# A state-space tokenizer before attention and a feed-forward layer: part of its chunk loop moved from VectorE and ScalarE to GpSimd

## The chip, the cores and the metric

The kernel runs on one NeuronCore of a Trainium2 chip, as one launch. The metric is device microseconds of one execution; lower is better. The median of three runs of the kernel before is given below. The profile is of one further execution, taken by the hardware profiler.

## What is computed

The reference is a vision tower's one layer: a tokenizer that builds the hidden states, then `h + attention(layernorm(h))` (local, landmark and global attention), then a feed-forward layer with block-wise quantized operands. The change lies in the tokenizer alone, which is, cut to what matters:

```python
C = x[..., 0] + 1j * x[..., 1]                    # (16, 256, 64)
B = B_ri[..., 0] + 1j * B_ri[..., 1]
A = -exp(inv_A_real) + 1j * A_imag
dt = exp(log_dt)
dtA = A * dt[:, None]
Ct = B[None] * C / (1.0 - dtA / 2) * dt[:, None]
dA = (1.0 + dtA / 2) / (1.0 - dtA / 2)
V = exp(log(dA)[:, :, None] * arange(512))         # (256, 64, 512)
h = 2.0 * einsum('chn,hnl->chl', Ct, V).real       # (16, 256, 512)
```

For every token h (256 of them) this is a product of the 16 x 64 coefficients with the 64 x 512 powers, in complex numbers.

## The kernel before

The whole program is a row of stages with a barrier of all engines between two of them: tokenizer, local attention, landmark attention, landmarks from tokens, landmark keys, global attention, feed-forward. Each stage has its own block of instructions per engine; in a stage the engines are tied by semaphores written out by hand. Nothing is scheduled by a planner: each engine runs its instructions in the order of the code, and a wait in front of an instruction holds back all that is behind it on that engine.

The tokenizer (`tokenizer`, from L115) splits the power l: with l = a + 64 b, a in 0..63 and b in 0..7, the power of a is the right operand of a matmul and the power of b is folded into the left one. The state index n and the two parts (real, imaginary) make the 128 partitions that are summed over. After a start that forms the parameters (VectorE, L293 to L349), transposes them and x (TensorE) and prepares the tables `X`, `Pb` (the coefficients times the powers of b, L382 to L387) and `ER` (the decay of the powers of a, L375, L240), the loop goes over 16 chunks (`NCH`) of 16 tokens (`CH`):

- ScalarE, `phases` (L247): 16 instructions of 64 elements, the turn a times omega of each token, into `ph`;
- ScalarE, `rounded` (L256): one instruction of 1024 elements that adds 1.5 x 2^23 to it, so that f32 rounds it to a whole number, into `nf`;
- VectorE, `fractions` (L394): takes the constant off again and subtracts `ph`, so `nf` holds the negative fraction of a turn (scalar_tensor_tensor, 1024 elements);
- ScalarE (L274): the sine of it, in place;
- VectorE: the left operands `L`, two products of 2048 elements for the two parts (L403, both operands broadcast, out of `X` and `Pb`) and their sum (L408);
- VectorE (L411): the right operands `R`, sine times decay, 1024 elements;
- TensorE (L442): 16 f32 matmuls of 128 x 128 by 128 x 64, one a token (each shows as two records), into two PSUM banks;
- ScalarE, `tokens` (L264): two copies of the banks to `hs`, and a DMA of 512 KB on SP's queue (L203) stores them to `h_s`.

`ph`, `nf`, `L`, `R`, `hs` and the pairs of banks have two buffers each. The orders on the engines are: VectorE `fractions(0)`, then for each chunk the two products, the sum, the decay product, `fractions(ch + 1)`; ScalarE `phases(0)`, `rounded(0)`, then for each chunk the sine, `phases(ch + 1)`, `rounded(ch + 1)`, `tokens(ch - 1)`. TensorE waits for `l_ready` and `r_ready` of a chunk before its first token. GpSimd has no instruction in this stage; it works in local attention (L724 to L742), global attention (L1752 to L1775) and the feed-forward layer (L2184).

Of the kernel before, what the change touches and what calls it, by code (L numbers as in the profile page):

```python
# [7 lines left out]
ALU = mybir.AluOpType  # L8
ACT = mybir.ActivationFunctionType
# [6 lines left out]
P = 128  # L16
BATCH = 16
# [17 lines left out]
ROUND = 1.5 * 2.0 ** 23  # L35
# [80 lines left out]
def tokenizer(nc, A, consts_d, h_d):  # L116


    CH = 16
    NCH = TOK // CH  # L120
    ctx = ExitStack()
    with ctx:
        def sb(name, shape, dt=F32):
            return ctx.enter_context(nc.sbuf_tensor(name, shape, dt))

        def sem(name):
            return nc.alloc_semaphore(name)
# [5 lines left out]
        aim = sb("tk_aim", [P, 2, NST])  # L133
        bri = sb("tk_bri", [P, 2, NST, 2])
        nat = sb("tk_nat", [P, 29, 2, NST])
        big = sb("tk_big", [P, 1])
        cst64 = sb("tk_c64", [P, 3, TOK])
        par = sb("tk_par", [P, 4, TOK])
        X = sb("tk_x", [P, 2, TOK, BATCH])
        ER = sb("tk_er", [P, TOK, 64])  # L140
        W = sb("tk_w", [P, 2, TOK, 8])
        Pb = sb("tk_pb", [P, 2, TOK, 8])
        L = sb("tk_l", [P, 2, 2, CH, P])

        WA, WB = (L[:, k, 0].rearrange("p t (m b) -> p (t m) b", b=8) for k in range(2))
        ph, nf = (xin[:, k].rearrange("p c n -> p (c n)").rearrange("p (u t a) -> p u t a", u=2, t=CH)
                  for k in range(2))
        R, hs = (W[:, k].rearrange("p t b -> p (t b)").rearrange("p (u t a) -> p u t a", u=2, t=CH)
                 for k in range(2))
# [22 lines left out]
        s_ev = sem("tk_ev")  # L172
        s_er0 = sem("tk_er0")
        s_er = sem("tk_er1")
        s_wph = sem("tk_wph")
        s_wsn = sem("tk_wsn")
        s_pb = sem("tk_pbd")
        ph_ready = sem("tk_ph_ready")
        rr_ready = sem("tk_rr_ready")
        nf_ready = sem("tk_nf_ready")  # L180
        sin_ready = sem("tk_sin_ready")
        r_ready = sem("tk_r_ready")
        l_ready = sem("tk_l_ready")
        mm_ready = sem("tk_mm_ready")
        hs_ready = sem("tk_hs_ready")
        out_done = [sem(f"tk_out_done{u}") for u in range(2)]
# [21 lines left out]
        @block.scalar  # L208
        def _(act):

            act.wait_ge(s_ld, 80)
            act.activation(nat[:, 0, 0, 0:2], ldt[:], ACT.Exp).then_inc(s_act, 1)
            act.activation(nat[:, 1], iar[:], ACT.Exp).then_inc(s_act, 1)

            act.wait_ge(s_nat, 1)
            act.activation(nat[:, 10], nat[:, 9], ACT.Ln).then_inc(s_act, 1)
            act.wait_ge(s_nat, 2)
            act.activation(nat[:, 11], nat[:, 12], ACT.Arctan).then_inc(s_act, 1)

            act.wait_ge(s_x, 32)  # L220
            for ri in range(2):
                for a in range(2):
                    src = xin[:, a].rearrange("p c (n r) -> p c n r", r=2)[:, :, :, ri]
                    for e in range(2):
                        ins = act.activation(xdup[:, ri, a, :, e * NST:(e + 1) * NST], src, ACT.Copy)
                    ins.then_inc(s_xd, 1)
            for k in range(16):
                ri, q, a = k // 8, k % 4, (k % 8) // 4
                act.wait_ge(s_xtr, k + 1)
                act.activation(X[:, ri, a * P:(a + 1) * P, 4 * q:4 * q + 4],  # L230
                               ps[(k + 2) % 8][:].rearrange("p (q t) -> p t q", q=4), ACT.Copy).then_inc(s_ev, 1)

            for w in range(2):
                act.wait_ge(s_wph, 2 + w)
                act.activation(W[:, w], W[:, w], ACT.Sin, scale=-TWO_PI, bias=tau[:, 1 + w:2 + w]).then_inc(s_wsn, 1)
            act.wait_ge(s_wph, 1)
            act.activation(WA, WA, ACT.Exp).then_inc(s_wsn, 1)
            for k in range(8):
                act.wait_ge(s_er0, k + 1)
                act.activation(ER[:, 32 * k:32 * k + 32], ER[:, 32 * k:32 * k + 32], ACT.Exp).then_inc(s_er, 1)  # L240

            def phases(ch):

                if ch >= 2:
                    act.wait_ge(nf_ready, ch - 1)
                for t in range(CH):
                    ins = act.activation(ph[:, ch % 2, t], c("iota_a"), ACT.Identity,  # L247
                                         scale=par[:, 1, ch * CH + t:ch * CH + t + 1], bias=c("off_r"))
                ins.then_inc(ph_ready, 1)

            def rounded(ch):

                act.wait_ge(ph_ready, ch + 1)
                if ch >= 2:
                    act.wait_ge(r_ready, ch - 1)
                act.activation(nf[:, ch % 2], ph[:, ch % 2], ACT.Identity, bias=big[:]).then_inc(rr_ready, 1)  # L256

            def tokens(ch):

                act.wait_ge(mm_ready, ch + 1)  # L260
                if ch >= 2:
                    act.wait_ge(out_done[ch % 2], 16 * (ch // 2))
                for k in range(2):
                    ins = act.activation(hs[:, ch % 2, 8 * k:8 * k + 8], ps[ch % 2 * 2 + k][:].rearrange(  # L264
                        "p (t a) -> p t a", t=8), ACT.Copy)
                ins.then_inc(hs_ready, 1)

            act.wait_ge(s_xd, 4)
            act.wait_ge(s_par, 2)
            phases(0)  # L270
            rounded(0)
            for ch in range(NCH):
                act.wait_ge(nf_ready, ch + 1)
                act.activation(nf[:, ch % 2], nf[:, ch % 2], ACT.Sin, scale=-TWO_PI  # L274
                               ).then_inc(sin_ready, 1)
                if ch + 1 < NCH:
                    phases(ch + 1)
                    rounded(ch + 1)
                if ch:
                    tokens(ch - 1)  # L280
            tokens(NCH - 1)

        @block.vector
        def _(dve):
            st = Steps(dve, s_dve)
# [3 lines left out]
                    n = st.mark(f(a))  # L289
                return n  # L290

            st.mark(dve.memset(big[:], ROUND))
            dve.wait_ge(s_act, 2)  # L293
            dt = nat[:, 0, 0, 0:2]
            hdt, ear, zr, zi = nat[:, 2, 0, 0:2], nat[:, 1], nat[:, 3], nat[:, 4]
# [95 lines left out]
            def fractions(ch):  # L391

                dve.wait_ge(rr_ready, ch + 1)
                dve.scalar_tensor_tensor(nf[:, ch % 2], nf[:, ch % 2], ROUND, ph[:, ch % 2], ALU.subtract, ALU.subtract  # L394
                                         ).then_inc(nf_ready, 1)

            fractions(0)
            for ch in range(NCH):
                t0, u = ch * CH, ch % 2
                if ch >= 2:  # L400
                    dve.wait_ge(mm_ready, ch - 1)
                for k in range(2):
                    ins = dve.tensor_tensor(L[:, u, k].rearrange("p t (c b) -> p t c b", b=8),  # L403
                                            X[:, k, t0:t0 + CH, :, None].to_broadcast([P, CH, BATCH, 8]),
                                            Pb[:, k, t0:t0 + CH, None, :].to_broadcast([P, CH, BATCH, 8]), ALU.mult)
                    st.mark(ins)
                st.wait(st.n)
                dve.tensor_tensor(L[:, u, 0], L[:, u, 0], L[:, u, 1], ALU.add).then_inc(l_ready, 1)  # L408
                dve.wait_ge(sin_ready, ch + 1)
                dve.wait_ge(s_er, ch // 2 + 1)  # L410
                dve.tensor_tensor(R[:, u], nf[:, u], ER[:, t0:t0 + CH], ALU.mult).then_inc(r_ready, 1)  # L411
                if ch + 1 < NCH:
                    fractions(ch + 1)

        @block.tensor
        def _(pe):

            pe.wait_ge(s_nat, 3)
            for a in range(2):
                for q in range(4):  # L420
                    ins = pe.transpose(ps[a][:, q * P:(q + 1) * P], dup4[:, q, a], ident)
                ins.then_inc(s_tr, 1)
            for k in range(16):
                ri, q, a = k // 8, k % 4, (k % 8) // 4
                pe.wait_ge(s_xd, ri * 2 + a + 1)
                if k >= 8:
                    pe.wait_ge(s_ev, k - 7)
                elif k >= 6:
                    pe.wait_ge(s_par, k - 5)
                for j in range(4):  # L430
                    ins = pe.transpose(ps[(k + 2) % 8][:, j * P:(j + 1) * P], xdup[:, ri, a, 4 * q + j], ident)
                ins.then_inc(s_xtr, 1)
            pe.wait_ge(s_ev, 16)
            for ch in range(NCH):
                u = ch % 2
                pe.wait_ge(l_ready, ch + 1)
                pe.wait_ge(r_ready, ch + 1)
                if ch >= 2:
                    pe.wait_ge(hs_ready, ch - 1)
                for t in range(CH):  # L440
                    o = ps[u * 2 + t // 8][:, (t % 8) * 64:(t % 8) * 64 + 64]
                    ins = pe.matmul(o, L[:, u, 0, t], R[:, u, t], start=True, stop=True)  # L442
                ins.then_inc(mm_ready, 1)
# [1937 lines left out]
```

## Time and profile before

| | us |
|---|---|
| median of 3 runs | 1784.9 (1778.79 to 1786.39) |
| the profiled execution | 1778.12 |
| its span, first to last instruction | 1776.3 |
| VectorE busy | 1307.3 (74%) |
| TensorE busy | 1508.6 (85%) |
| ScalarE busy | 1022.3 (58%) |
| GpSimd busy | 561.2 (32%), none of it in the tokenizer but four memsets at 0.3 us |
| tokenizer, up to its last store's issue | 0 to 224 |

The span is 1.8 us less than the execution's own time. TensorE's granted clock is 0.893 over the whole span, in tenths by slice of 44.4 us 8555569999999999999976689889999899999999; 0.50 is 1.2 GHz and 1.00 is 2.4 GHz. In rows of the trace the engines are PE (TensorE matmul), PEld (its weight load), DVE (VectorE), ACT (ScalarE), POOL (GpSimd) and SP; a trailing q is an engine's queue, and L442 is line 442 of the kernel. An engine's gap before an instruction stands in brackets with what ended it. x16 is a count of instructions merged into a row. The names of buffers are those of the memory that a tile lies in: `ph` and `nf` show as tk_xin, `R` and `hs` as tk_w.

### The profile page before, as it was taken

The numbers are of one execution on the slowest core, as the hardware profiler recorded it, in microseconds if no ns is written. First come the engines' busy times: TensorE is split into PE (matmuls) and PEld (weight loads), VectorE is DVE, ScalarE is ACT, GpSimd is POOL, SyncE is SP. The second block draws the span as 40 slices with busy tenths as digits, with TensorE's granted clock in tenths as the row PEclk, the third lists the DMA queues.
The fourth block names the chain that finished last, engine by engine and source line by source line (L and its number), as shares of the span: only waits on it lengthen the run. The fifth ranks groups of instructions, "written<-read, shape, count | busy, mean of one in ns | idle before, by whom it ended". The sixth has DMA issues, their size and how long they took to land. (4 is left out here: it accounts for less than half of the span.)

```text
span 1776.3 us, 33180 instructions
## 1 busy us (share of the span) xinstructions
PE 1508.6 (85%) x11568; PEld 1007.3 (57%) x11568; DVE 1307.3 (74%) x2414; ACT 1022.3 (58%) x2579; POOL 561.2 (32%) x584
## 2 busy tenths in 40 slices
PE   2177739999999999999958776679999589999997
PEld 2177726766776677667646755456666334444443
DVE  8999836777777777777614255169999579999997
ACT  7799627888778887888722133056776232333232
POOL 0000014445444444454400000025555523333333
PEclk8555569999999999999976689889999899999999
DMA  2022251222222222222230065345555124444443
GB/s 59 1 60 60 59 168 67 100 97 77 77 101 77 89 77 97 100 77 77 85 131 1 0 221 188 111 138 163 163 163 163 60 66 104 98 102 100 107 96 89
DMA packets 189649, 171.82 MB, mean 97 GB/s; under 512 B 120064, under 2 KB 121728, under 8 KB 189568
## 3 DMA queue, kind: packets, MB, share of 16 engines
q1 hardware_dynamic: 189568, 170.80, 32.7%
q8 instruction: 44, 0.72, 0.2%
q14 instruction: 37, 0.30, 0.1%
HBM read 94.21 MB, written 59.77 MB: 87 GB/s over the span
## 5 line engine op out<-in xcount | busy, mean ns | idle before, releaser
L1057 PE MATMUL al_ps<-al_w,al_xT 128*128 128x512 f32 (+2 forms) x1024 | 352.0, 498 | 0.0
L1057 PEld LDWEIGHTS al_ps<-al_w,al_xT 128*128 128x128 f32 x1024 | 192.6, 193 | 127.4 <-issue 107.3
L2184 POOL TENSOR_TENSOR ff_zq<-ff_z,ff_back 128x1024 bf16<-128x1024 fp8e4 x64 | 122.4, 1912 | 225.8 <-DVE ff_z L2207 225.8
L442 PE MATMUL tk_ps<-tk_w,tk_l 128*128 128x64 f32 x512 | 113.0, 422 | 79.5 <-DVE tk_w L411 52.4
L442 PEld LDWEIGHTS tk_ps<-tk_w,tk_l 128*128 128x128 f32 x512 | 110.4, 332 | 82.1 <-issue 82.1
L2151 ACT ACTIVATE ff_sg<-ff_gate 128x1024 f32<-128x1024 f32 x64 | 65.6, 1025 | 149.1 <-PE ff_gate L2230 149.1
L739 POOL TENSOR_TENSOR al_qv<-al_qv,al_qe 128x512 f32<-128x512 f32 x48 | 62.0, 1291 | 248.7 <-PE al_ps L1130 248.7
L2249 PE MATMUL ff_acc<-wdT,ff_zT 128*128 128x512 bf16 x512 | 122.5, 383 | 5.5 <-DMA ff_zT<-ff_zq 5.5
L2230 PE MATMUL ff_up<-wuT,xqT 128*128 128x512 bf16 x512 | 121.6, 380 | 3.0 <-DVE ff_z L2199 3.0
L2230 PE MATMUL ff_gate<-wgT,xqT 128*128 128x512 bf16 x512 | 121.9, 381 | 0.7 <-ACT ff_sg L2151 0.7
L993 DVE TENSOR_REDUCE al_mx<-al_ps 128x32 f32<-128x2048 f32 x32 | 73.3, 2292 | 58.1 <-PE al_ps L1130 58.1
L1994 PE MATMUL ag_ps<-ag_w,ag_aT 128*128 128x512 f32 x256 | 114.8, 602 | 0.0
L885 ACT ACTIVATE al_p<-al_ps,al_mx 128x64 f32<-128x64 f32 x512 | 107.8, 355 | 0.0
L724 POOL TENSOR_TENSOR al_qk<-al_r 128x512 f32<-128x512 f32 x64 | 81.7, 1288 | 68.1 <-DVE al_r L933 68.1
L1762 POOL TENSOR_TENSOR ag_a<-ag_a,ag_o 128x1024 f32<-128x1024 f32 x16 | 37.7, 2357 | 167.0 <-DVE ag_a L1913 167.0
L2249 PEld LDWEIGHTS ff_acc<-wdT,ff_zT 128*128 128x128 bf16 x512 | 50.1, 98 | 68.0 <-DMA ff_zT<-ff_zq 7.4
L247 ACT ACTIVATE tk_xin<-tk_cst,tk_par 128x64 f32<-128x64 f32 x256 | 86.3, 425 | 0.0
L2230 PEld LDWEIGHTS ff_gate<-wgT,xqT 128*128 128x128 bf16 x512 | 50.3, 98 | 62.4 <-issue 1.9
L2230 PEld LDWEIGHTS ff_up<-wuT,xqT 128*128 128x128 bf16 x512 | 45.0, 98 | 71.2 <-DVE ff_z L2199 25.4
L2199 DVE TENSOR_TENSOR ff_z<-ff_sg,ff_up 128x1024 f32<-128x1024 f32 x64 | 77.7, 1214 | 9.8 <-ACT ff_sg L2151 9.8
L2204 DVE TENSOR_TENSOR ff_zv<-ff_z,ff_inv 128x1024 f32<-128x1024 f32 x64 | 78.5, 1226 | 2.2
L1994 PEld LDWEIGHTS ag_ps<-ag_w,ag_aT 128*128 128x128 f32 x256 | 48.6, 195 | 54.8 <-issue 54.8
(311 smaller groups left out, 3413.3 us busy)
## 6 DMA issues: line engine op xcount, KB each, us to landing
al_hx<-h_s SPq DMA_DIRECT2D x36, 256.0 KB, 2.7
o_s<-al_o SPq DMA_DIRECT2D x32, 272.0 KB, 2.1
h_s<-tk_w SPq DMA_DIRECT2D x16, 512.0 KB, 3.8
v_s<-al_v SPq DMA_DIRECT2D x32, 256.0 KB, 2.1
k_s<-al_kT SPq DMA_DIRECT2D x32, 256.0 KB, 2.4
q_s<-al_qT SPq DMA_DIRECT2D x32, 256.0 KB, 2.6
lt_kT<-k_s SPq DMA_DIRECT2D x16, 512.0 KB, 4.6
lt_v<-v_s SPq DMA_DIRECT2D x16, 512.0 KB, 3.6
```

The costliest lines, as they stand in the source:

```text
L247: ins = act.activation(ph[:, ch % 2, t], c("iota_a"), ACT.Identity, scale=par[:, 1, ch * CH + t:ch * CH + t + 1], bias=c("off_r"))
L442: ins = pe.matmul(o, L[:, u, 0, t], R[:, u, t], start=True, stop=True)
L724: pool.tensor_tensor(qk[:, part * D:(part + 1) * D].rearrange("p (h d) -> p h d", d=DH), r1[:, heads], r2[:, heads], ALU.add).then_inc(out ...
L885: ins = act.activation(p[:, g, hd * S:(hd + 1) * S], ps[:, g, hd * S:(hd + 1) * S], ACT.Exp, bias=mx[:, 8 * g + hd:8 * g + hd + 1])
L993: dve.tensor_reduce(mx[:], ps[:, 0:4].rearrange("p b (h s) -> p (b h) s", s=S), AX.X, ALU.max, negate=True).then_inc(mx_r.sem, 1)
L1057: ins = pe.matmul(out, xT[:, T, k], w[:, k, cols], start=False, stop=True, skip_group_check=True)
L1994: ins = pe.matmul(out, aT[:, T, k], w[:, k], start=False, stop=True, skip_group_check=True)
L2184: pool.tensor_tensor(zq[:, u].rearrange("p (k s) -> p k s", s=QB), z8[:, u].rearrange("p (k s) -> p k s", s=QB), back[:, u, :, None].to_br ...
L2199: dve.tensor_tensor(z[:, u], sg[:, u], up[:].rearrange("p b n -> p (b n)"), ALU.mult).then_inc(z_r.sem, 1)
L2204: ls(dve.tensor_tensor(b3_(zv[:]), b3_(z[:, u]), inv[:, :, None].to_broadcast([P, NB, QB]), ALU.mult))
L2230: ins = pe.matmul(bank[:, n], K.xqT[:, k, bass.ds(t * P, P)], wT[:, k, (2 * hf + n) * D:(2 * hf + n + 1) * D], start=(k == 0), stop=(k == ...
L2249: ins = pe.matmul(acc[:, T], zT[:, u, k], K.wdT[:, 2 * KC * hf + k], start=False, stop=True, skip_group_check=True)
```

## The change

`CV = 13` splits a chunk's 16 tokens. VectorE forms the left operands of the first 13; GpSimd forms those of the last three (`left`: two products and their sum, on 384 elements each) with a semaphore of its own, `lp_ready`, which TensorE waits for in front of token 13. GpSimd also takes the product with the decay (for all 16 tokens) from VectorE, and the rounding from ScalarE (`rounded`, now a tensor_scalar with the constant as immediate, so that the tile `big` goes). ScalarE computes the phases two chunks ahead of the sine in place of one. GpSimd's order is `rounded(0)`, `rounded(1)`, `left(0)`, then for each chunk the decay product, `left(ch + 1)`, `rounded(ch + 2)`. The waits on buffers are those of before, moved with the work.

```diff
--- before.py
+++ after.py
@@ -117,6 +117,7 @@
 
 
     CH = 16
+    CV = 13
     NCH = TOK // CH
     ctx = ExitStack()
     with ctx:
@@ -133,7 +134,6 @@
         aim = sb("tk_aim", [P, 2, NST])
         bri = sb("tk_bri", [P, 2, NST, 2])
         nat = sb("tk_nat", [P, 29, 2, NST])
-        big = sb("tk_big", [P, 1])
         cst64 = sb("tk_c64", [P, 3, TOK])
         par = sb("tk_par", [P, 4, TOK])
         X = sb("tk_x", [P, 2, TOK, BATCH])
@@ -181,6 +181,8 @@
         sin_ready = sem("tk_sin_ready")
         r_ready = sem("tk_r_ready")
         l_ready = sem("tk_l_ready")
+        lp_ready = sem("tk_lp_ready")
+        s_pool = sem("tk_pool")
         mm_ready = sem("tk_mm_ready")
         hs_ready = sem("tk_hs_ready")
         out_done = [sem(f"tk_out_done{u}") for u in range(2)]
@@ -248,13 +250,6 @@
                                          scale=par[:, 1, ch * CH + t:ch * CH + t + 1], bias=c("off_r"))
                 ins.then_inc(ph_ready, 1)
 
-            def rounded(ch):
-
-                act.wait_ge(ph_ready, ch + 1)
-                if ch >= 2:
-                    act.wait_ge(r_ready, ch - 1)
-                act.activation(nf[:, ch % 2], ph[:, ch % 2], ACT.Identity, bias=big[:]).then_inc(rr_ready, 1)
-
             def tokens(ch):
 
                 act.wait_ge(mm_ready, ch + 1)
@@ -268,14 +263,13 @@
             act.wait_ge(s_xd, 4)
             act.wait_ge(s_par, 2)
             phases(0)
-            rounded(0)
+            phases(1)
             for ch in range(NCH):
                 act.wait_ge(nf_ready, ch + 1)
                 act.activation(nf[:, ch % 2], nf[:, ch % 2], ACT.Sin, scale=-TWO_PI
                                ).then_inc(sin_ready, 1)
-                if ch + 1 < NCH:
-                    phases(ch + 1)
-                    rounded(ch + 1)
+                if ch + 2 < NCH:
+                    phases(ch + 2)
                 if ch:
                     tokens(ch - 1)
             tokens(NCH - 1)
@@ -289,7 +283,6 @@
                     n = st.mark(f(a))
                 return n
 
-            st.mark(dve.memset(big[:], ROUND))
             dve.wait_ge(s_act, 2)
             dt = nat[:, 0, 0, 0:2]
             hdt, ear, zr, zi = nat[:, 2, 0, 0:2], nat[:, 1], nat[:, 3], nat[:, 4]
@@ -400,17 +393,54 @@
                 if ch >= 2:
                     dve.wait_ge(mm_ready, ch - 1)
                 for k in range(2):
-                    ins = dve.tensor_tensor(L[:, u, k].rearrange("p t (c b) -> p t c b", b=8),
-                                            X[:, k, t0:t0 + CH, :, None].to_broadcast([P, CH, BATCH, 8]),
-                                            Pb[:, k, t0:t0 + CH, None, :].to_broadcast([P, CH, BATCH, 8]), ALU.mult)
+                    ins = dve.tensor_tensor(L[:, u, k, 0:CV].rearrange("p t (c b) -> p t c b", b=8),
+                                            X[:, k, t0:t0 + CV, :, None].to_broadcast([P, CV, BATCH, 8]),
+                                            Pb[:, k, t0:t0 + CV, None, :].to_broadcast([P, CV, BATCH, 8]), ALU.mult)
                     st.mark(ins)
                 st.wait(st.n)
-                dve.tensor_tensor(L[:, u, 0], L[:, u, 0], L[:, u, 1], ALU.add).then_inc(l_ready, 1)
-                dve.wait_ge(sin_ready, ch + 1)
-                dve.wait_ge(s_er, ch // 2 + 1)
-                dve.tensor_tensor(R[:, u], nf[:, u], ER[:, t0:t0 + CH], ALU.mult).then_inc(r_ready, 1)
+                dve.tensor_tensor(L[:, u, 0, 0:CV], L[:, u, 0, 0:CV], L[:, u, 1, 0:CV], ALU.add).then_inc(l_ready, 1)
                 if ch + 1 < NCH:
                     fractions(ch + 1)
+
+        @block.gpsimd
+        def _(pool):
+            st = Steps(pool, s_pool)
+
+            def rounded(ch):
+
+                pool.wait_ge(ph_ready, ch + 1)
+                if ch >= 2:
+                    pool.wait_ge(r_ready, ch - 1)
+                pool.tensor_scalar(nf[:, ch % 2], ph[:, ch % 2], ROUND, None, ALU.add).then_inc(rr_ready, 1)
+
+            def left(ch):
+
+                t0, u, n = ch * CH + CV, ch % 2, CH - CV
+                if ch >= 2:
+                    pool.wait_ge(mm_ready, ch - 1)
+                for k in range(2):
+                    st.mark(pool.tensor_tensor(L[:, u, k, CV:].rearrange("p t (c b) -> p t c b", b=8),
+                                               X[:, k, t0:t0 + n, :, None].to_broadcast([P, n, BATCH, 8]),
+                                               Pb[:, k, t0:t0 + n, None, :].to_broadcast([P, n, BATCH, 8]), ALU.mult))
+                st.wait(st.n)
+                pool.tensor_tensor(L[:, u, 0, CV:], L[:, u, 0, CV:], L[:, u, 1, CV:], ALU.add).then_inc(lp_ready, 1)
+
+            rounded(0)
+            rounded(1)
+            pool.wait_ge(s_pb, 1)
+            pool.wait_ge(s_ev, 16)
+            left(0)
+            for ch in range(NCH):
+                u = ch % 2
+                pool.wait_ge(sin_ready, ch + 1)
+                pool.wait_ge(s_er, ch // 2 + 1)
+                if ch >= 2:
+                    pool.wait_ge(mm_ready, ch - 1)
+                pool.tensor_tensor(R[:, u], nf[:, u], ER[:, ch * CH:(ch + 1) * CH], ALU.mult).then_inc(r_ready, 1)
+                if ch + 1 < NCH:
+                    left(ch + 1)
+                if ch + 2 < NCH:
+                    rounded(ch + 2)
 
         @block.tensor
         def _(pe):
@@ -438,6 +468,8 @@
                 if ch >= 2:
                     pe.wait_ge(hs_ready, ch - 1)
                 for t in range(CH):
+                    if t == CV:
+                        pe.wait_ge(lp_ready, ch + 1)
                     o = ps[u * 2 + t // 8][:, (t % 8) * 64:(t % 8) * 64 + 64]
                     ins = pe.matmul(o, L[:, u, 0, t], R[:, u, t], start=True, stop=True)
                 ins.then_inc(mm_ready, 1)
```

## Rows read from the trace of the kernel before

**Rows 1.** Windows of the tokenizer's chunk loop, busy us and instructions of each engine:
```profile
core 0: us, PE busy (x) PEld busy (x) DVE busy (x) ACT busy (x) POOL busy (x), PEclk, DMA share, GB/s
144.00:189.00 45.00, 35.30 (x161) 34.51 (x162) 44.83 (x26) 42.41 (x101) 0.00 (x0) 0.50 0.29 59
216.00:224.00 8.00, 6.89 (x32) 6.71 (x32) 0.00 (x0) 1.07 (x2) 0.00 (x0) 0.50 0.31 65
```

**Rows 2.** Timeline of one chunk: start us, us, engine, line, operation, tiles, count:
```profile
152.65 1.22 DVE L394 SCALAR_TENSOR_TENSOR tk_xin<-tk_xin 128x1024 f32<-128x1024 f32 x1
152.84 7.06 PE L442 MATMUL tk_ps<-tk_w,tk_l 128*128 128x64 f32 x32 [1.94 <-issue]
...
153.79 4.49 DVE L403 TENSOR_TENSOR tk_l<-tk_x,tk_pb 128x2048 f32<-128x2048 f32 x2
153.90 1.06 ACT L274 ACTIVATE tk_xin<-tk_xin 128x1024 f32<-128x1024 f32 x1 [0.49 <-DVE tk_xin L394]
154.87 5.39 ACT L247 ACTIVATE tk_xin<-tk_cst,tk_par 128x64 f32<-128x64 f32 x16
158.31 2.29 DVE L408 TENSOR_TENSOR tk_l<-tk_l 128x2048 f32<-128x2048 f32 x1
160.29 1.15 ACT L256 ACTIVATE tk_xin<-tk_xin,tk_big 128x1024 f32<-128x1024 f32 x1
160.52 1.22 DVE L411 TENSOR_TENSOR tk_w<-tk_xin,tk_er 128x1024 f32<-128x1024 f32 x1
161.35 1.07 ACT L264 ACTIVATE tk_w<-tk_ps 128x512 f32<-128x512 f32 x2
161.65 1.22 DVE L394 SCALAR_TENSOR_TENSOR tk_xin<-tk_xin 128x1024 f32<-128x1024 f32 x1
```

**Rows 3.** Timeline, the start of the loop and its last chunk:
```profile
55.45 5.39 ACT L247 ACTIVATE tk_xin<-tk_cst,tk_par 128x64 f32<-128x64 f32 x16
58.06 2.29 DVE L382 TENSOR_TENSOR tk_pb<-tk_w,tk_par 128x2048 f32<-128x2048 f32 x1
...
71.65 1.22 DVE L394 SCALAR_TENSOR_TENSOR tk_xin<-tk_xin 128x1024 f32<-128x1024 f32 x1
...
80.88 7.06 PE L442 MATMUL tk_ps<-tk_w,tk_l 128*128 128x64 f32 x32 [50.43 <-DVE tk_w L411]
...
215.84 7.06 PE L442 MATMUL tk_ps<-tk_w,tk_l 128*128 128x64 f32 x32 [1.94 <-issue]
```

**Rows 4.** GpSimd's groups by form: busy us, mean ns of one | idle before:
```profile
L740 POOL TENSOR_TENSOR al_qv<-al_qv,al_qe 128x512 f32<-128x512 f32 x48 | 60.9, 1270 | 3.8
L731 POOL TENSOR_TENSOR al_qv<-al_qwt,al_qinv 128x512 f32<-128x512 f32 x48 | 49.1, 1052 | 27.5 <-DVEq L951 27.5
L1762 POOL TENSOR_TENSOR ag_a<-ag_a,ag_o 128x1024 f32<-128x1024 f32 x16 | 37.7, 2357 | 167.0 <-DVE ag_a L1913 167.0
L1752 POOL TENSOR_TENSOR ag_xv<-ag_xn,ag_inv 128x1024 f32<-128x1024 f32 x16 | 30.6, 1914 | 69.3 <-DVEq L1950 69.3
...
L1772 POOL TENSOR_SCALAR ag_t<-ag_t 128x2 f32<-128x2 f32 x48 | 9.3, 193 | 4.2
...
L713 POOL MEMSET al_vbd<- 128x2176 f32 x1 | 1.9, 1912 | 231.5 <-POOLq L2298 231.5
L1404 POOL MEMSET lt_pT<- 128x1024 f32 x1 | 1.0, 952 | 0.0
```

**Rows 5.** Timeline of two overlaps in global attention, then two lines' min/median/max ns:
```profile
1298.24 2.36 POOL L1762 TENSOR_TENSOR ag_a<-ag_a,ag_o 128x1024 f32<-128x1024 f32 x1 [0.51 <-DVE ag_a L1913]
...
1307.78 1.18 POOL L1771 TENSOR_TENSOR ag_t<-ag_t,ag_ve 128x2 f32<-128x2 f32 x1
...
1299.35 1.33 DVE L1900 TENSOR_TENSOR ag_sm<-ag_sm,ag_floor 128x64 f32<-128x64 f32 x1
...
1307.68 1.22 DVE L1958 TENSOR_TENSOR ag_xq<-ag_x,ag_back 128x1024 bf16<-128x1024 fp8e4 x1
...
L1900 DVE TENSOR_TENSOR ag_sm<-ag_sm,ag_floor x16: 225/1332/1803, 1160.5 to 1372.6; 128x64 f32<-128x64 f32 x16
...
L1771 POOL TENSOR_TENSOR ag_t<-ag_t,ag_ve x48: 196/197/1186, 1188.9 to 1412.5; 128x2 f32<-128x2 f32 x48
```

## Prediction

> **What bounds the kernel now.** I read first the page's busy shares by slice, to find the stage that the change touches: the tokenizer, the first 224 us. Then the windows of its chunk loop [rows 1]: in 45 us, which is five chunks, VectorE is busy for 44.83 us, ScalarE for 42.41, TensorE for 35.30 at a granted clock of 0.50 (the lower level, 1.2 GHz), and GpSimd for nothing. So VectorE sets the pace, with ScalarE not far behind. The timeline of one chunk says the same instruction by instruction [rows 2]: from one L394 to the next (152.65 to 161.65) are 9.00 us, and in them VectorE does the subtraction that gives the fraction (L394, 1.22 us), two products of 2048 elements (L403, 4.48 together), their sum (L408, 2.29) and the product with the decay (L411, 1.22), with no gap. ScalarE's only idle time is 0.49 us before the sine (L274). The first matmul of the loop starts at 80.88 and that of chunk 15 at 215.84 [rows 3]: 15 periods of 9.00. The time of the stage is a start, 15 periods and an end of one chunk of matmuls and its store.
>
> **What the change takes off, engine by engine.** VectorE: L411 goes (1.22 us). Its other three big instructions shrink from 16 to 13 tokens, 2048 to 1664 elements. From 1.22 us for 1024 elements and 2.29 for 2048 [rows 2] an element costs 1.045 ns, so 1664 cost 1.89 us. What is left: 3 x 1.89 + 1.22 = 6.89 us by single durations. ScalarE: L256 goes (1.15 us, of which 1.05 show in the spacing of the rows, from 160.29 to the L264 at 161.35 [rows 2]). What is left is 9.00 - 0.49 - 1.05 = 7.46 us. That phases run two chunks ahead costs ScalarE nothing: the same 16 instructions, issued one chunk earlier, behind the same sine. The constant's memset on VectorE is 0.06 us at the very start and I cost it at nothing.
>
> **What it puts on GpSimd.** The trace has GpSimd tensor-tensor rows of 1024 and 512 elements [rows 4]. Two full f32 operands: 2357 ns for 1024 (L1762) and 1270 for 512 (L740), so 2.12 ns per element and 384 elements (three tokens) cost 1.00 us. One operand broadcast: 1914 and 1052 ns (L1752, L731), 1.68 ns per element, 384 cost 0.84 us. The product with the decay is 1024 full elements: 2.36 us. The two small products, each with broadcast operands, take 0.84 each (at most 1.00, if a pattern broadcast on both sides runs as two full operands); their sum 1.00. The rounding is a tensor-scalar of 1024 elements, which the trace has only at 2 elements (L1772, 193 ns). Its floor is a memset of 1024 elements, which reads nothing: 952 ns (L1404); its ceiling the two-operand 2.36 us. I take 1.05, near the floor, because it has one operand to read and one to write: the memset's 0.83 ns per element (952 against 1912 ns for 2176 elements, L713) plus the 0.19 of the smallest instruction. The Trainium skill ("GPSIMD Engine Reference", section on engine selection) says one-input work on GpSimd runs roughly at line rate; by it, an estimate at one element per 1.2 GHz cycle, the rounding's streaming would be 0.85 us and the sum the same within 1 us for the whole loop. No row here tests it. GpSimd's sum per chunk: 2.36 + 0.84 + 0.84 + 1.00 + 1.05 = 6.09 us.
>
> Side by side, VectorE with 6.9, ScalarE 7.46, TensorE 7.1 and GpSimd 6.1 would all be under 9.00, and the period would be ScalarE's. That sum is right only if VectorE and GpSimd can work at once.
>
> **Why I do not believe they can.** In the global attention stage the trace has both engines reading SBUF at the same time [rows 5]. GpSimd's L1762 runs from 1298.24 to 1300.60. VectorE's L1900, an f32 tensor-tensor of 64 elements with both operands in SBUF, starts at 1299.35 and ends at 1300.68: it took 1.33 us where its fastest took 0.225. Its median over 16 is 1332 ns, so this is its rule. The other way round: VectorE's L1958, both operands in SBUF, runs from 1307.68 to 1308.90; GpSimd's L1771, two elements, starts at 1307.78 and ends at 1308.96, 1.18 us where its median is 0.197. Each waits for the other's end, whoever came first. All four VectorE instructions that remain in the loop (L403 twice, L408, L394) have two SBUF operands, as L1900 and L1958 do, and all five of GpSimd's read SBUF. So 9 instructions a chunk would take turns. The Trainium skill states this as a rule ("SBUF — State Buffer", section "Who interferes with whom"): a VectorE instruction with two SBUF inputs and a GpSimd one that reads SBUF hold the shared ports exclusively, and the second blocks fully. Taken with whole durations, it would give 6.89 + 6.09 = 12.98 us a period and +64 us in all; the rows are a little kinder, as follows.
>
> **The sum.** In the two overlaps the blocked instruction ended 0.08 and 0.06 us behind the other, not its own 0.225 or 0.197 behind it: 0.14 us of its fixed part is hidden at each hand-over. In the likely order of a chunk (product with decay, fraction, small product, big product, small product, big product, small sum, big sum, rounding) there are 8 hand-overs, 1.12 us. The period is 12.98 - 1.12 = 11.86 us. Nothing else is late in such a period: GpSimd's order asks for the sine of chunk n+1, which ScalarE (7.46 of 11.86) has long done; the wait for the matmuls of chunk n-1, 7.1 us of work that starts at the end of the product with the decay, is over before the chunk's small products; behind the added matmul wait at token 13 only 3 tokens are queued, and the small sum was done before the decay product of the same chunk. The stores that SP issues wait for ScalarE's copies as before, one a chunk, with more time between them.
> - 15 periods: 15 x (11.86 - 9.00) = +42.9 us.
> - The start: phases 0 end at 60.84 (55.45 + 5.39) [rows 3], phases 1 some 5.4 later; both roundings fall into VectorE's chain of two-operand instructions (L382 to L387, the first row of it in [rows 3]) that ends where L394 starts, at 71.65, and push it by about 0.95 each, +1.9. From there the first chunk's fraction, three small, three big instructions and the decay product take 1.22 + 2.68 + 5.67 + 2.36 - 7 x 0.14 = 10.95 us, so the first matmul starts at 84.5 instead of 80.88: +3.6 with the push.
> - The end: in the last two chunks there is nothing left to round: -1.8.
> Together +44.7, say +45 us. The stages behind start in the same state (the last matmuls of the loop run at the lower clock now [rows 1] and will with longer gaps between them), none of their instructions changes, and I cost them at nothing. The profiled execution took 1778.1 us (span 1776.3, 1.8 around it), so it becomes 1823; the median of the three runs shown is 1784.9, 6.8 above it, and the median becomes 1830.
>
> Ends of the unknowns, per chunk and times 16: hand-overs that hide nothing, +1.12, +18 us; rounding at its ceiling, +1.3, +21; small products at 1.00, +0.3, +5; the scalar-tensor-tensor L394, a form which no row shows blocked, running free of the lock, -1.1 to -1.2, -19. They give +26 to +89.
>
> **The rivals.**
> - **The lock costs its full price or more** (chance 0.15): hand-overs hide nothing and the rounding is dear. Period 13 to 14.3, +63 to +84 us, 1848 to 1869. For it: the hidden 0.14 is measured on tiny instructions only. Against: both rows agree to 0.01.
> - **A part escapes it** (0.12): L394 does not take part, or hand-overs hide more. Period near 10.7, +26 us, 1811.
> - **Long streams run side by side** (0.07), the case on the other side. The blocked instructions of rows 5 are short; if two long ones could share the ports, the period is ScalarE's 7.46 us and the first matmul starts when VectorE has done its own left part, near 78.4: 15 x (7.46 - 9.00) - 2.5 = -25.6 us, 1759. It decides from the point where more than 4.0 of GpSimd's 6.09 us run under VectorE's cover (12.98 - 4.0 = 9.0), of which the hand-overs give only 1.12. Against: L1762, which blocks, is itself a long one of 2.36 us, and L1958, which blocks the other way, is 1.22.
> - **A draw** (0.02): just that much cover, the period stays 9.
>
> **How the numbers follow.** The forecast (the turn-taking at 11.5 to 12.5 us a period, 1822 to 1840) has 0.64. About 0.5% of this kernel, 9 us, is what a measurement can tell from no change. Faster by more than that: 0.07; within: 0.03, the draw and a little of the weakest escape; slower: 0.90. The range reaches from 1808 (+23, the escape and some spread) to 1868 (+83, the full price); outside are the two cases without a lock, 0.09, and tails of the others.
>
> **What would show it.** In the changed profile: L411's successor and the small products on GpSimd; a period between the first matmuls of two chunks near 11.9 us; VectorE's big products of 1664 elements far over 1.89 us on average, its "busy" share still near full although it has less to do; GpSimd's instructions likewise over their 0.84, 1.00 and 2.36. TensorE idle for nearly 5 us a chunk, ScalarE for 4. If the big products average 1.89 us and the period is near 7.5, the lock is wrong. If they are stretched and the period is 13 or more, the price of a turn or of the rounding was. If the loop is as predicted and the total isn't, a later stage has moved.

## The result, and the profile after

The changed kernel takes 1848.3 us (median of 4 runs, 1844.29 to 1854.47) against 1785.6 (4 runs): ratio 1.0372, 95% interval 1.034 to 1.0403. It is slower. The forecast was 1830 with a range of 1808 to 1868; the direction held, and so did the mechanism, two engines that take turns; one term was mis-sized.

The profiled execution has a span of 1842.5 us, 66.2 more than before. First the loop's windows, in the columns of [rows 1]:

```profile
144.00:189.00 45.00, 22.46 (x102) 21.79 (x102) 35.17 (x14) 24.51 (x64) 44.77 (x17) 0.50 0.18 39
```

GpSimd, which did nothing here before, is busy for 44.77 of 45 us, VectorE for 35.17, ScalarE for 24.51 and TensorE for 22.46. On its face that is a kernel bound by a slow GpSimd. The timeline of one chunk, which answers to [rows 2], shows why that reading is too quick. L396 and L401 are VectorE's big products and sum, now of 1664 elements, L387 the fraction; L422 and L426 are GpSimd's small products and sum, L439 the decay product (sine times decay), L414 the rounding:

```profile
108.72 2.34 POOL L439 TENSOR_TENSOR tk_w<-tk_xin,tk_er 128x1024 f32<-128x1024 f32 x1
108.78 3.35 DVE L387 SCALAR_TENSOR_TENSOR tk_xin<-tk_xin 128x1024 f32<-128x1024 f32 x1 [2.66 <-POOL tk_xin L414]
111.02 4.28 POOL L422 TENSOR_TENSOR tk_l<-tk_x,tk_pb 128x384 f32<-128x384 f32 x2
...
111.16 7.06 PE L474 MATMUL tk_ps<-tk_w,tk_l 128*128 128x64 f32 x32 [6.42 <-issue]
112.06 4.98 DVE L396 TENSOR_TENSOR tk_l<-tk_x,tk_pb 128x1664 f32<-128x1664 f32 x2
112.17 1.06 ACT L269 ACTIVATE tk_xin<-tk_xin 128x1024 f32<-128x1024 f32 x1 [6.21 <-DVE tk_xin L387]
...
115.38 2.53 POOL L426 TENSOR_TENSOR tk_l<-tk_l 128x384 f32<-128x384 f32 x1
117.08 2.58 DVE L401 TENSOR_TENSOR tk_l<-tk_l 128x1664 f32<-128x1664 f32 x1
117.87 4.41 POOL L414 TENSOR_SCALAR tk_xin<-tk_xin 128x1024 f32<-128x1024 f32 x1
...
122.25 2.34 POOL L439 TENSOR_TENSOR tk_w<-tk_xin,tk_er 128x1024 f32<-128x1024 f32 x1
```

Read the ends (start plus duration), not the durations. GpSimd's decay product ends at 111.06; VectorE's fraction, which started at 108.78, ends at 112.13, 1.07 us behind it. GpSimd's small sum ends at 117.91, 0.87 behind the big product's end at 117.04; VectorE's sum at 119.66, 1.75 behind that; the rounding at 122.28, 2.62 behind that. Every instruction ends its own length, less a little, behind the end of the other engine's last one: turns. The turns add up to 2.34 + 1.07 + 4.91 (two small and two big products, 112.13 to 117.04) + 0.87 + 1.75 + 2.62 = 13.56, and the period, 108.72 to 122.25, is 13.53. (Of the rounding's 2.62 only a part keeps VectorE out; e2 below.) A large part of a row's duration here is waiting (the fraction's row has 3.35 us where it had 1.22 before), so "44.77 busy" of GpSimd is no measure of its work.

The ends of the loop, against [rows 3]:

```profile
60.80 4.25 POOL L414 TENSOR_SCALAR tk_xin<-tk_xin 128x1024 f32<-128x1024 f32 x1 [60.37 <-ACT tk_xin L249]
62.34 3.12 DVE L377 TENSOR_TENSOR tk_pb<-tk_w,tk_par 128x2048 f32<-128x2048 f32 x1
...
67.70 3.00 DVE L379 TENSOR_TENSOR tk_pb<-tk_pb,tk_l 128x2048 f32<-128x2048 f32 x1
...
84.14 7.06 PE L474 MATMUL tk_ps<-tk_w,tk_l 128*128 128x64 f32 x32 [54.56 <-POOL tk_w L439]
...
259.98 7.06 PE L474 MATMUL tk_ps<-tk_w,tk_l 128*128 128x64 f32 x32 [6.46 <-issue]
...
273.51 7.06 PE L474 MATMUL tk_ps<-tk_w,tk_l 128*128 128x64 f32 x32 [6.47 <-issue]
...
284.30 7.06 PE L474 MATMUL tk_ps<-tk_w,tk_l 128*128 128x64 f32 x32 [3.73 <-issue]
```

The first matmul came 3.3 us later than before, the last chunk's 68.5 us later (284.30 against 215.84). The last period, without a rounding, was 10.79; the one before it (259.98 to 273.51) still had one and was 13.53. The next stage, local attention, begins with the statistics of a layer norm, here before (L914) and after (L946): count, shortest, median and longest in ns, first and last start in us, form.

```profile
L914 DVE BATCH_NORM_STATS2 al_bn<-al_hx x34: 673/680/695, 235.4 to 845.5; 128x6 f32<-128x512 f32 x34
L946 DVE BATCH_NORM_STATS2 al_bn<-al_hx x34: 673/682/695, 304.2 to 913.4; 128x6 f32<-128x512 f32 x34
```

They start at 304.2 instead of 235.4, 68.8 later; the rest of the program took 1538.3 us instead of 1540.9. All of the loss is in the tokenizer: 3.3 us before the first matmul, the rest in the loop.

The times of that rest need a word, because the runs below differ in it. No kernel of this study changes an instruction behind the tokenizer, yet from local attention's first statistics to the end it took 1538 to 1555 us in the profiled executions. In 66 us of landmark attention the granted clock was anything from 0.63 to 0.78. So each experiment is judged by its period and by when local attention starts; the total is given beside them. Where only one execution was timed, the text says so. Why the rest varies stays open.

### The profile page after: what moved, and what is told of

Read it like the earlier page. It is cut to its first block and busy times, and to the rows that moved or that the text cites. A ratio compares the mean times of both kernels' runs of the same rounds, so it can differ in the third digit from the quotient of the medians.

```text
span 1842.5 us, 33226 instructions
## 1 busy us (share of the span) xinstructions
PE 1503.5 (82%) x11568; PEld 1000.8 (54%) x11568; DVE 1336.8 (73%) x2397; ACT 1003.4 (54%) x2563; POOL 779.0 (42%) x664
## 5 line engine op out<-in xcount | busy, mean ns | idle before, releaser
L414 POOL TENSOR_SCALAR tk_xin<-tk_xin 128x1024 f32<-128x1024 f32 x16 | 70.2, 4385 | 61.4 <-ACT tk_xin L249 61.4
L2281 PEld LDWEIGHTS ff_acc<-wdT,ff_zT 128*128 128x128 bf16 x512 | 50.5, 99 | 68.8 <-DMA ff_zT<-ff_zq 7.2
L249 ACT ACTIVATE tk_xin<-tk_cst,tk_par 128x64 f32<-128x64 f32 x256 | 86.2, 425 | 0.0
```

The lines of the kernel that those rows point to most:

```text
L2281: ins = pe.matmul(acc[:, T], zT[:, u, k], K.wdT[:, 2 * KC * hf + k], start=False, stop=True, skip_group_check=True)
```

## Experiments

**The rounding back on ScalarE** (e1_round_back), the other two moves kept, and phases one chunk ahead again as before:

```diff
-                pool.tensor_scalar(nf[:, ch % 2], ph[:, ch % 2], ROUND, None, ALU.add).then_inc(rr_ready, 1)
+                act.activation(nf[:, ch % 2], ph[:, ch % 2], ACT.Identity, bias=big[:]).then_inc(rr_ready, 1)
```

> The changed kernel with the rounding put back on ScalarE (and phases one chunk ahead, as before). Theory (GpSimd and VectorE take turns at SBUF, and the rounding as a GpSimd tensor_scalar holds up a turn of 2.63 us, from the end of VectorE's sum at 92.59+13.53n to its own end): the period falls from 13.53 by 2.63 to about 10.9 us, the kernel to about 1808 us in the profiled execution, still slower than before. Rival (the decay product and the small products are what is dear, the rounding is hidden): the period stays above 12.5 us.

Timeline of one chunk (L440 decay product, L397 fraction):

```profile
154.12 3.98 POOL L440 TENSOR_TENSOR tk_w<-tk_xin,tk_er 128x1024 f32<-128x1024 f32 x1
...
156.00 3.19 DVE L397 SCALAR_TENSOR_TENSOR tk_xin<-tk_xin 128x1024 f32<-128x1024 f32 x1
...
164.92 3.99 POOL L440 TENSOR_TENSOR tk_w<-tk_xin,tk_er 128x1024 f32<-128x1024 f32 x1
```

The period is 10.80, local attention starts at 264.2 (40.0 earlier than in the changed kernel), the kernel takes 1811.2 us, ratio to before 1.0146 (1.0123 to 1.0168). The profiled execution took 1814.5 us where about 1808 was expected: the period is even a little shorter than the expected 10.9, but the rest of the program took 1548.5 us, 10.2 more than in the changed kernel. So the rounding accounts for over half of the loss (40.0 of 68.8 us), and the rest of the change is still a loss by itself: local attention starts 28.8 us later than before.

**Only the rounding on GpSimd** (e2_round_only): the kernel before with that one line moved and phases two ahead.

```diff
-                act.activation(nf[:, ch % 2], ph[:, ch % 2], ACT.Identity, bias=big[:]).then_inc(rr_ready, 1)
+                pool.tensor_scalar(nf[:, ch % 2], ph[:, ch % 2], ROUND, None, ALU.add).then_inc(rr_ready, 1)
```

> The kernel before with only the rounding moved to GpSimd (phases two chunks ahead). VectorE has its full 9.00 us a chunk. If the GpSimd tensor_scalar keeps VectorE from SBUF for its whole 2.63 us, the period is about 11.5 us (+37 us in all). If it keeps it out only for the part in which it reads (the two roundings ahead of the loop delayed L377 and L379 by only 0.84 and 0.72 us), the period is about 9.8 us (+12). If there is no turn-taking at all, 9.0.

Timeline (L413 rounding, L386 fraction, L395 the two big products, L403 decay product):

```profile
160.50 1.22 DVE L386 SCALAR_TENSOR_TENSOR tk_xin<-tk_xin 128x1024 f32<-128x1024 f32 x1
...
160.74 3.61 POOL L413 TENSOR_SCALAR tk_xin<-tk_xin 128x1024 f32<-128x1024 f32 x1 [6.23 <-DVE tk_w L403]
161.64 5.32 DVE L395 TENSOR_TENSOR tk_l<-tk_x,tk_pb 128x2048 f32<-128x2048 f32 x2
...
170.34 1.22 DVE L386 SCALAR_TENSOR_TENSOR tk_xin<-tk_xin 128x1024 f32<-128x1024 f32 x1
```

The rounding waits for the fraction's end (161.72) and ends 2.63 us behind it, at 164.35. The products take 5.32 us instead of 4.49: held up by 0.83, no more, and they run on while the rounding is still at work. The period is 9.84, the one execution took 1794.9 us, local attention starts 12.8 us later than before. So the rounding is 2.63 us long, but only 0.83 of it is a turn. In the changed kernel the other 1.8 us cost as much, because VectorE's next instruction there, the fraction, needs the result: the 2.66 us of idle in its row above.

**GpSimd writes but does not read** (e3_write_only): each of its instructions in the loop becomes two memsets of its output tile. Left out are the left operands of three tokens, the rounding and the decay product; the sine's scale is made tiny.

```diff
-                pool.tensor_tensor(R[:, u], nf[:, u], ER[:, ch * CH:(ch + 1) * CH], ALU.mult).then_inc(r_ready, 1)
+                st(pool.memset(R[:, u], 1.0))
+                pool.memset(R[:, u], 1.0).then_inc(r_ready, 1)
```

> The changed kernel with each GpSimd instruction of the loop replaced by two memsets of the same output tile, one waiting for the other: GpSimd keeps its place in every chain of waits and stays busy for some 6 us a chunk, but reads nothing. What is left out: the left operands of three tokens, the rounding and the decay product (and the sine's scale is made tiny). Theory (reads of SBUF are what the two engines take turns at): VectorE's instructions are back at 1.89 and 1.22 us, and the period is ScalarE's, about 7.5 us; the tokenizer ends near 200 us instead of 292. Rival (the longer chain of semaphores through GpSimd, not the ports): the period stays over 11 us although nothing is read.

Timeline (L396, L401, L387 as in the changed kernel, L440 and L441 the decay product's memsets), then the windows:

```profile
159.94 0.95 POOL L440 MEMSET tk_w<- 128x1024 f32 x1
160.22 1.22 DVE L387 SCALAR_TENSOR_TENSOR tk_xin<-tk_xin 128x1024 f32<-128x1024 f32 x1
160.95 0.95 POOL L441 MEMSET tk_w<- 128x1024 f32 x1
161.89 3.69 DVE L396 TENSOR_TENSOR tk_l<-tk_x,tk_pb 128x1664 f32<-128x1664 f32 x2 [0.46 <-PE tk_ps L476]
...
169.10 3.69 DVE L396 TENSOR_TENSOR tk_l<-tk_x,tk_pb 128x1664 f32<-128x1664 f32 x2 [0.46 <-PE tk_ps L476]
```
```profile
99.00:144.00 45.00, 44.97 (x211) 44.81 (x211) 44.27 (x27) 45.00 (x120) 39.72 (x67) 0.50 0.32 71
```

With the same chain of waits through GpSimd, and GpSimd busy for 39.72 of 45 us, the fraction is back at 1.22 us and the two products at 3.69, and the period is 7.21 us; local attention starts at 202.7, and the one execution took 1752.3 us. VectorE overlaps GpSimd's memsets without a trace of waiting. The rival, the longer chain of semaphores, is out: what the engines take turns at is reading SBUF. The expected 7.5 was a little high: ScalarE's spacings close up when it never waits, and TensorE is now full too.

**Only the decay product on GpSimd** (e5_decay_only), the rest as before.

```diff
-                dve.tensor_tensor(R[:, u], nf[:, u], ER[:, t0:t0 + CH], ALU.mult).then_inc(r_ready, 1)
+                pool.tensor_tensor(R[:, ch % 2], nf[:, ch % 2], ER[:, ch * CH:(ch + 1) * CH], ALU.mult).then_inc(r_ready, 1)
```

> The kernel before with only the decay product moved to GpSimd. Without turn-taking VectorE would need 7.8 us a chunk and ScalarE's 8.5 us would be the period (-8 us in all). Theory: VectorE's 7.8 us and GpSimd's 2.34 less 0.1 add up, period about 10.0 us, +15 us in all: a product that costs VectorE 1.22 costs 2.3 on GpSimd with VectorE standing still.

Timeline (L419 is the decay product on GpSimd, L403 the two big products):

```profile
152.49 6.65 DVE L403 TENSOR_TENSOR tk_l<-tk_x,tk_pb 128x2048 f32<-128x2048 f32 x2
...
153.74 3.25 POOL L419 TENSOR_TENSOR tk_w<-tk_xin,tk_er 128x1024 f32<-128x1024 f32 x1 [6.78 <-ACT tk_xin L274]
...
162.51 6.65 DVE L403 TENSOR_TENSOR tk_l<-tk_x,tk_pb 128x2048 f32<-128x2048 f32 x2
```

The products take 6.65 us instead of 4.49 [rows 2], the period is 10.02. VectorE was rid of an instruction of 1.22 us and stood still for 2.16. Local attention starts 15.8 us later than before, as expected; the one execution took 1808.2 us, 24.6 over the median of before (1783.6). That is more than 15.8 because the rest of the program took 1555.1 us here against 1540.9.

**One operand in PSUM** (e4_one_psum_operand): e5 with `Pb[:, 0]` in four PSUM banks that the loop leaves free, and the product that reads it done second.

```diff
-            st(dve.tensor_tensor(Pb[:, 0], Pb[:, 0], WA, ALU.add))
+            st(dve.tensor_tensor(Pb0[:], Pb[:, 0].rearrange("p t b -> p (t b)"), WA.rearrange("p t b -> p (t b)"), ALU.add))
...
-                for k in range(2):
+                for k in (1, 0):
+                    pb = Pb[:, k] if k else Pb0[:].rearrange("p (t b) -> p t b", b=8)
```

> The kernel with only the decay product on GpSimd (period 10.02), and one more edit: the table Pb's first part is written to four free PSUM banks (the sum before the loop writes there, at no cost), so that one of VectorE's two products a chunk has one operand in SBUF and one in PSUM; it is done second, when the sine is ready for GpSimd. Theory (the turn is taken per SBUF operand, not per engine): GpSimd's 2.34 us run beside that product, VectorE needs some 7.8 to 8.0 us a chunk and ScalarE's 8.5 us is the period; the tokenizer is 7 to 8 us shorter than before, the kernel about 1776 us, 0.4% under before. Rival (any VectorE instruction stands still while GpSimd reads): the period stays near 10.0.

Timeline (L406 the two big products, L422 the decay product on GpSimd, L411 the big sum, L396 the fraction):

```profile
152.08 4.48 DVE L406 TENSOR_TENSOR tk_l<-tk_x,tk_pb 128x2048 f32<-128x2048 f32 x2
...
153.33 3.25 POOL L422 TENSOR_TENSOR tk_w<-tk_xin,tk_er 128x1024 f32<-128x1024 f32 x1 [5.58 <-ACT tk_xin L276]
156.60 2.29 DVE L411 TENSOR_TENSOR tk_l<-tk_l 128x2048 f32<-128x2048 f32 x1
...
159.77 1.23 DVE L396 SCALAR_TENSOR_TENSOR tk_xin<-tk_xin 128x1024 f32<-128x1024 f32 x1 [0.88 <-ACT tk_xin L258]
160.91 4.48 DVE L406 TENSOR_TENSOR tk_l<-tk_x,tk_pb 128x2048 f32<-128x2048 f32 x2
```

The same decay product, and VectorE's pair is at 4.48 again: GpSimd waits out the first product (to about 154.3), then reads for 2.25 us beside the second, which has one operand in PSUM. So whether VectorE takes a turn hangs on where its operands lie: with one of the two in PSUM, it does not. The Trainium skill ("SBUF — State Buffer", "Who interferes with whom") says that outside VectorE's two-port modes an instruction of it with at most one SBUF input does not contend with GpSimd, and that one with two contends only with GpSimd instructions that read SBUF. The trace agrees with the first here (4.48 for the pair) and with the second in e3 (1.22 and 3.69). The period is 8.83, not the expected 8.5, and local attention starts 4.0 us earlier than before, not 7 to 8. VectorE waits 0.88 us for the rounding in front of the fraction: sine, phases, rounding and fraction of one chunk follow each other in a ring, which e8 opens. The kernel takes 1775.5 us, ratio to before 0.9965 (0.9947 to 0.9982).

**The price of the rounding** (e6_round_two_operands): the changed kernel with the rounding as a two-operand instruction, and three probes with VectorE idle behind the loop.

```diff
-                pool.tensor_scalar(nf[:, ch % 2], ph[:, ch % 2], ROUND, None, ALU.add).then_inc(rr_ready, 1)
+                pool.tensor_tensor(nf[:, ch % 2], ph[:, ch % 2], big[:, :, None].to_broadcast([P, CH, 64]), ALU.add
+                                   ).then_inc(rr_ready, 1)
```

> The changed kernel with the rounding written as a GpSimd tensor_tensor with a broadcast constant in place of a tensor_scalar, and, after the loop with VectorE idle, three each of a tensor_scalar of 1024 elements, of 512 elements, and a copy of 1024, to price them by themselves. Theory (the tensor_scalar is dear in itself, 2.63 us, of which only some 0.85 keep VectorE out): alone it also takes 2.6 us, and the two-operand form, 1.91 alone, ends 1.8 us behind VectorE's sum, so the period falls from 13.53 to about 12.7 us. Rival (the tensor_scalar takes 1.05 us alone and is stretched by VectorE): alone 1.05, and the period does not fall.

GpSimd's timeline: the last rounding (L416) and decay product, then the probes, three of each:

```profile
256.90 3.54 POOL L416 TENSOR_TENSOR tk_xin<-tk_xin,tk_big 128x1024 f32<-128x1024 f32 x1
260.40 2.33 POOL L443 TENSOR_TENSOR tk_w<-tk_xin,tk_er 128x1024 f32<-128x1024 f32 x1
...
273.50 8.47 POOL L451 TENSOR_SCALAR tk_x<-tk_er 128x1024 f32<-128x1024 f32 x3
282.05 4.63 POOL L453 TENSOR_SCALAR tk_x<-tk_er 128x512 f32<-128x512 f32 x3
286.74 3.24 POOL L455 COPY tk_x<-tk_er 128x1024 f32<-128x1024 f32 x3
```

With nobody else reading, a tensor_scalar of 1024 elements takes 2.82 us a piece, waits between them included (8.47 for three; a single row has 2.77), one of 512 elements 1.54 (1.49), a copy of 1024 elements 1.08 (1.04). The 2.63 us of the loop are the 2.77 less the 0.14 of a hand-over: VectorE does not stretch the rounding. With the two-operand rounding the period is 12.65 (L443 from 159.25 to 171.90) against the expected 12.7: on GpSimd the instruction with one operand less is the dearer one. The one execution took 1842.3 us, with some 4 us for the probes in it: from the last chunk's matmul to local attention are 23.9 us here, 19.9 in the changed kernel.

**The rounding earlier in GpSimd's order** (e7_round_earlier), else the changed kernel.

```diff
+                if ch + 2 < NCH:
+                    rounded(ch + 2)
                 if ch + 1 < NCH:
                     left(ch + 1)
-                if ch + 2 < NCH:
-                    rounded(ch + 2)
```

> The changed kernel with one exchange in GpSimd's order: the rounding of chunk n+2 right behind the decay product of chunk n, ahead of the small products of chunk n+1. As changed, VectorE has nothing left but the fraction that waits for the rounding, so its whole 2.63 us are on the path though only some 0.85 of them keep VectorE from SBUF. Theory: issued earlier, the other 1.78 us run under VectorE's products; period 13.53 - 1.78 = about 11.75 us, the profiled execution about 1819 us. Rival (the whole 2.63 us are a turn): the period stays at 13.5.

Timeline (lines as in the changed kernel):

```profile
153.83 6.55 DVE L396 TENSOR_TENSOR tk_l<-tk_x,tk_pb 128x1664 f32<-128x1664 f32 x2 [0.93 <-PE tk_ps L474]
154.64 3.99 POOL L439 TENSOR_TENSOR tk_w<-tk_xin,tk_er 128x1024 f32<-128x1024 f32 x1
...
158.79 4.22 POOL L414 TENSOR_SCALAR tk_xin<-tk_xin 128x1024 f32<-128x1024 f32 x1 [0.16 <-POOL tk_w L439]
160.41 2.61 DVE L401 TENSOR_TENSOR tk_l<-tk_l 128x1664 f32<-128x1664 f32 x1
162.98 2.63 POOL L422 TENSOR_TENSOR tk_l<-tk_x,tk_pb 128x384 f32<-128x384 f32 x2
...
165.82 6.55 DVE L396 TENSOR_TENSOR tk_l<-tk_x,tk_pb 128x1664 f32<-128x1664 f32 x2 [0.93 <-PE tk_ps L474]
```

The period is 11.99 instead of 13.53, 0.24 over the expected 11.75. VectorE has a new wait of 0.93 us for TensorE in front of its products; about 0.7 of it lie beside GpSimd's small products (L422, to 165.61), which VectorE would have waited out anyway, and the rest is about what is missing. Local attention starts 21.6 us earlier than in the changed kernel. The kernel takes 1831.8 us, ratio to before 1.0268 (1.0231 to 1.0304). The profiled execution took 1832.7 us where 1819 was expected: 10.0 of the 13.7 lie in the rest of the program, 1548.3 us here against 1538.3, and some 3.4 in the fourteen periods of 0.24 more. One exchange of two lines thus takes back nearly a third of the tokenizer's loss, and confirms that 1.8 us of the rounding are not a turn.

**The PSUM operand, with ScalarE's ring opened** (e8_psum_two_ahead): e4 with phases two chunks ahead and the rounding right behind the sine.

```diff
             phases(0)
+            phases(1)
             rounded(0)
...
                 if ch + 1 < NCH:
-                    phases(ch + 1)
                     rounded(ch + 1)
+                if ch + 2 < NCH:
+                    phases(ch + 2)
```

> The kernel with one product operand in PSUM and the decay product on GpSimd (period 8.83), and ScalarE's order changed: phases two chunks ahead, and the rounding of chunk n+1 right behind the sine of chunk n. In the 8.83 both ScalarE (0.32 us) and VectorE (0.88 us) have gaps, because sine, phases, rounding and fraction of one chunk follow each other in a ring (0.96 + 5.43 + 1.18 + 1.26 = 8.83). Theory: the ring is opened, the period is ScalarE's work, 8.5 us, and the tokenizer another 4 to 5 us shorter, the kernel about 1771 us, 0.6% under before. Rival (the period is VectorE's turns with GpSimd): it stays at 8.8.

Timeline (L277 sine, L258 rounding, L249 phases, L266 copies of the tokens, L413 VectorE's sum):

```profile
153.83 1.12 ACT L266 ACTIVATE tk_w<-tk_ps 128x512 f32<-128x512 f32 x2
154.78 1.11 ACT L277 ACTIVATE tk_xin<-tk_xin 128x1024 f32<-128x1024 f32 x1
...
155.73 1.20 ACT L258 ACTIVATE tk_xin<-tk_xin,tk_big 128x1024 f32<-128x1024 f32 x1
...
156.77 5.47 ACT L249 ACTIVATE tk_xin<-tk_cst,tk_par 128x64 f32<-128x64 f32 x16
157.81 2.68 DVE L413 TENSOR_TENSOR tk_l<-tk_l 128x2048 f32<-128x2048 f32 x1
...
163.02 1.12 ACT L277 ACTIVATE tk_xin<-tk_xin 128x1024 f32<-128x1024 f32 x1
```

ScalarE has no gap left and the period is its own work, 8.24 us, less than the 8.5 that I had put down for it. VectorE has no gap either, but it does not set the pace: its sum has 2.68 us instead of 2.29 because the decay product is still running when it starts, and early in the loop, where it was not, VectorE's chunks were 7.86 us apart and ScalarE's already 8.23. Local attention starts at 221.0, 14.4 us earlier than before and 10.4 earlier than in e4, where 4 to 5 were expected. The kernel takes 1769.0 us, ratio to before 0.9921 (0.9902 to 0.9941): it beats both kernels.

## Why the prediction was right, and where it was off

- **Whether the two engines can work at once.** They can't, as forecast from two overlaps of small instructions [rows 5]; e3 shows it by taking GpSimd's reads away, e4 by taking one of VectorE's. The rival "long streams run side by side" is out.
- **The price of a turn.** The prediction had, per chunk, 2.36 for the decay product, 1.08 for the fraction, 4.90 for the two small and two big products, 0.86 and 1.75 for the sums. Measured: 2.34, 1.07, 4.91, 0.87, 1.75. The 0.14 us hidden at a hand-over carried over from instructions of 2 and 64 elements to ones of 1664.
- **L394 free of the lock** ("a part escapes it"): no. The fraction (L387) ends 1.07 us behind GpSimd's product, like the rest.
- **The term that failed: the rounding.** I took 1.05 us near the memset floor, less 0.14 at the hand-over, 0.91; it measured 2.62, above even the two-operand price of 2.36 that I had called its ceiling. Fourteen roundings in the loop at 1.71 more are 23.9 us, and the last matmuls were 68.5 - 44.7 = 23.8 later than forecast. That the two agree so well is partly luck: the forecast also took a rounding too many off at the end, as below, and other small errors made up for it. The reason given, one operand to read and one to write, holds for a copy (1.04 us in e6) and not for a tensor_scalar (2.77); why that is so dear stays open. What the sum called a turn, VectorE kept out of SBUF, was 0.83 us (e2), near the 0.91: it is the instruction's length that was wrong, and with it the wait for its result. The Trainium skill ("GPSIMD Engine Reference", "4.1 Engine selection") has one-input work at roughly line rate: the copy agrees, the tensor_scalar does not, and the measurement decides.
- **The start.** Forecast at 84.5 for the first matmul, measured at 84.14: the two early roundings held L377 and L379 up by 0.84 and 0.71 us, not 0.95 each.
- **The end.** Forecast at -1.8, two periods without a rounding. GpSimd's order has a rounding in 14 of the 15 periods, so only the last is without (10.79 against 13.53), and at the forecast's own price of 0.91 that is -0.9.
- **The full-price rival** named the right number (a period of 13 to 14.3, 1848 and up; measured 13.53 and 1848.3) for half the right reason: the rounding was dear, but the hand-overs were not.
- **Stages behind** at nothing: they gave back 2.6 us in the profiled execution, within what they vary by.
- **A step that I did not see:** that the rounding stands last in GpSimd's order, with VectorE waiting for it. With 0.91 us it would have mattered little; with 2.62, two thirds of it are time in which VectorE could have worked, which e7 mostly gives back. It also undid a sign that the prediction named: VectorE's busy share is not near full but 35.17 of 45 us, because it stands idle for the rounding.

## What to carry to other kernels

Before moving work from VectorE to an idle GpSimd, count the operands that both read from SBUF: if VectorE's instructions have two each, the moved work is paid in full, at GpSimd's price (2.2 us here for what took VectorE 1.2). What makes the move pay is an operand of VectorE's in PSUM at the time when GpSimd reads. Shown here for f32 instructions of the forms in this loop. And a busy share misleads where engines take turns: look at whether an instruction ends its own length behind its start or behind the other engine's end.

## What had not been expected of the hardware

- A GpSimd tensor_scalar (f32, immediate add) costs 2.5 ns per element (2.77 us for 1024, 1.49 for 512, in e6), against 1.91 us for a two-operand instruction with a broadcast [rows 4] and 1.04 for a copy.
- It keeps VectorE out for only 0.83 us (0.84 and 0.71 ahead of the loop, 0.83 in e2) of its 2.63. GpSimd's two-operand decay product keeps it out for all of its own (2.16 in e5, its 2.34 less a hand-over). The Trainium skill ("SBUF — State Buffer", "SBUF: two separate sides") has whichever starts first hold the ports for its whole instruction; this one did not hold them so long, and the measurement decides. Why stays open.
- In e3 TensorE is busy for 44.97 of 45.00 us and its granted clock stays at 0.50, the lower level, 1.2 GHz. In all kernels of this study the loop's windows from 99 to 189 us show it.
